# First batch's row sums and bias turn moved behind the high turn of token tile 2; the last product, its eviction and its store cut into two column halves

## The reference

```
x = x + tanh(g_xattn) * (fq(layernorm(x)) @ fq(ctx))             # fq: quantize to 0..255 and back
x = x + tanh(g_ffn)   * ffn(layernorm(x))
ffn(t):  gate = the 2 best of 16 experts for each row, from 2 of 4 groups, softmax scores + bias
         y    = sum over experts of gate_e * ((silu(t@w1_e + b1_e) * (t@w2_e + b2_e)) @ w3_e + b3_e)
         z    = (silu(t@sw1 + sb1) * (t@sw2 + sb2)) @ sw3 + sb3  # shared expert, 512 wide
         return y + z
```

## Time and profile before

| what | value |
|---|---|
| median of 3 runs | 316.2 us (315.91 to 316.38) |
| the profiled execution's own time | 316.27 us |
| its span | 314.3 us |
| PE busy | 293.9 us (94%) |
| DVE busy | 222.8 us (71%) |
| ACT busy | 114.9 us (37%) |
| mean granted TensorE clock | 0.998 of full speed |

### The profile page before, as it was taken

One profiled execution on the slowest core, in us unless ns is written; L12 is line 12 of the kernel. 1 busy time (PEld: TensorE's weight loads), 2 busy tenths in 40 slices (PEclk: granted clock), 3 DMA queues, 4 the chain that ended last, 5 costly groups with the idle time before them and its releaser, 6 DMA issues.

```text
span 314.3 us, 4647 instructions
## 1 busy us (share of the span) xinstructions
PE 293.9 (94%) x1868; PEld 149.4 (48%) x1868; DVE 222.8 (71%) x392; ACT 114.9 (37%) x130; POOL 24.3 (8%) x34
## 2 busy tenths in 40 slices
PE   0388999999999999999999999999999999999993
PEld 0224598954544445544444444444444444444441
DVE  2898987895898953685475988868784769659110
ACT  2998558769653540210343305302015040100000
POOL 2010200000002210000000011100101110000000
PEclk9999999999999999999999999999999999999999
DMA  7999970248710753000897600000000000600302
GB/s 277 413 325 346 301 219 6 82 136 168 230 60 0 136 106 95 2 2 0 250 306 250 229 39 2 0 0 0 2 0 0 2 1 0 255 15 1 133 33 104
DMA packets 35700, 35.56 MB, mean 113 GB/s; under 512 B 16068, under 2 KB 30428, under 8 KB 35548
## 3 DMA queue, kind: packets, MB, share of 16 engines
q1 hardware_dynamic: 35664, 35.23, 36.0%
q10 hardware_dynamic: 12, 0.00, 0.0%
HBM read 27.88 MB, written 4.20 MB: 102 GB/s over the span
## 4 chain that ended last, share of the span: by engine, by line
PE 83%; DVE 9%; DMA 3%; ACT 2%; SPq 1%; POOL 1%; issue 1%; DVEq 0%
PE PS L1532 26%; PE PS L1374 20%; PE PS L1565 12%; PE PS L1558 7%; PE PS L1409 7%; PE PS L1321 4%; DMA X<-in_x_dram 3%; PE PS L1390 2%; DVE stats L778 2%; PE PS L1398 2%; PE PS L1328 1%; DVE S2f L814 1%; POOL lnR L474 1%; DVE X L844 1%; DVE wrow L853 1%; DVE area L810 1%
## 5 line engine op out<-in xcount | busy, mean ns | idle before, releaser
L1374 PE MATMUL PS<-areaT,areaW 128*128 128x512 f16 x288 | 62.6, 379 | 0.0
L1374 PEld LDWEIGHTS PS<-areaT,areaW 128*128 128x128 f16 x288 | 28.0, 98 | 33.3
L1532 PE MATMUL PS<-areaT,area 128*128 128x512 f16 x192 | 42.1, 379 | 0.0
L1532 PE MATMUL PS<-areaT,areaW 128*128 128x512 f16 x192 | 42.1, 379 | 0.0
L1321 PE MATMUL PS<-area,areaQ 128*128 128x512 f16 x128 | 32.0, 400 | 1.6 <-DVE area L810 1.5
L1042 DVE SCALAR_TENSOR_TENSOR X<-PS,cf,X 128x512 f32<-128x512 f32 x22 | 15.5, 746 | 20.0 <-PE PS L1565 15.2
L1532 PEld LDWEIGHTS PS<-areaT,area 128*128 128x128 f16 x192 | 18.8, 98 | 22.7
L1532 PEld LDWEIGHTS PS<-areaT,areaW 128*128 128x128 f16 x192 | 18.8, 98 | 22.7
L778 DVE BATCH_NORM_STATS2 stats<-X 128x6 f32<-128x512 f32 x32 | 20.5, 683 | 4.5 <-DMA X<-in_x_dram 4.3
L1558 PE MATMUL PS<-SW,areaH 128*128 128x512 f16 x96 | 21.9, 379 | 0.0
L1321 PEld LDWEIGHTS PS<-area,areaQ 128*128 128x128 f16 x128 | 12.6, 102 | 17.8 <-DVE area L810 3.6
(11 more groups left out here) (187 smaller groups left out, 408.6 us busy)
## 6 DMA issues: line engine op xcount, KB each, us to landing
areaT<-in_ctx_dram SPq DMA_DIRECT2D x12, 512.0 KB, 8.1
ring<-in_L_ffn_sw_dram SPq DMA_DIRECT2D x12, 512.0 KB, 5.5
X<-in_x_dram SPq DMA_DIRECT2D x8, 512.0 KB, 7.6
ring<-in_L_ffn_ew_dram SPq DMA_DIRECT2D x16, 256.0 KB, 5.6
out_dram<-X SPq DMA_DIRECT2D x7, 512.0 KB, 2.7
ring<-in_ctx_dram SPq DMA_DIRECT2D x4, 512.0 KB, 3.8
ring<-in_L_ffn_ew_dram SPq DMA_DIRECT2D x2, 1024.0 KB, 5.0
areaQ<-gate_dram SPq DMA_DIRECT2D x1, 1024.0 KB, 6.8
```

Of the source, the lines that this page charges most:

```text
L1374: last = mm(PS[:, SU_BANK[half * SC + c] + w, lo:hi], SW[:, wp, 2 * c + w, k, :], XT[:, xp, k, tk], start=(k == 0 and n == 0), stop=(k == ...
L1532: last = mm(PS[:, EU_BANK[u] + w, :], W12S[j][:, wp, k, cs], XT[:, xp, k, b * S:(b + 1) * S], start=(k == 0 and n == 0), stop=(k == KC - 1 ...
```

## The change

1. On PE, `bias_columns` and `row_sums(0)` leave their place between the products of tile 2 (after k = 3) and are called in `transpose_tokens(2)`, between the high and the low turn. They wait for `at_read` 4 (the eviction of tile 3, which frees bank 3) in place of `q1_rdy`. PE no longer waits for `r1_rdy` and `sbT_rdy` before the products of tile 3.
2. On DVE, `row_terms(0)` and `shared_biases()` move from behind `attend(1)` to behind `ln2_lo(3)`; at the end of `shared_biases` DVE waits for its own two writes. `su_silu_of(0)` on ACT waits for them too, and the first DMA turn of the second batch (`turn_q1(4)`) also waits for the row sums.
3. The product `P3` of pair 1 of the second batch becomes two groups of 18 matmuls with 256 columns (`last_product`), the first in its old bank, the second in the next one (bank 4), each with a semaphore.
4. DVE evicts the two halves one by one (`last_halves`).
5. The stores of the last two tiles are five instead of three: the first 512 columns of tile 4 and of tile 5 as soon as `X11f` is done, the last 512 of tile 4 after `X12f` of pair 0, and the last 512 of tile 5 in two of 256 columns.

```
-            sp.wait_ge(y_rdy, evict_no(1, "X11f", 1))
-            store(TB + 1, slice(0, 512))
+            for pair in range(2):
+                sp.wait_ge(y_rdy, evict_no(1, "X11f", pair))
+                store(TB + pair, slice(0, 512))
             sp.wait_ge(y_rdy, evict_no(1, "X12f", 0))
-            store(TB)
+            store(TB, slice(512, D))
+            sp.wait_ge(y_first, 1)
+            store(TB + 1, slice(512, 768))
             sp.wait_ge(y_rdy, evict_no(1, "X12f", 1))
-            store(TB + 1, slice(512, D))
+            store(TB + 1, slice(768, D))
...
             attend(1)
-            row_terms(0)
-            shared_biases()
             lo_chunk("sw", 0)
...
             ln2_lo(3)
+            row_terms(0)
+            shared_biases()
             lo_chunk("sw", 4)
...
             def row_sums(b):
-                if b == 0:
-                    pe.wait_ge(q1_rdy, TB)
-                else:
+                if b:
                     for j in range(2):
                         pe.wait_ge(q1t_in[j], 32)
-                    pe.wait_ge(at_read, TB)
+                    pe.wait_ge(r1_rdy, 1)
+                    pe.wait_ge(sbT_rdy, 2)
...
                 pe.wait_ge(sbr_in, 32)
+                pe.wait_ge(at_read, TB)
                 nc.tensor.transpose(PS[:, 3, 8:16], sbr[:, :], idf[0:8, 0:8]).then_inc(sb_T, 1)
...
                 last.then_inc(tk_T, 1)
+                if i == 2:
+                    bias_columns()
+                    row_sums(0)
                 pe.wait_ge(ln_lo, i + 1)
...
                 products(2, k)
-                if k == 3:
-                    pe.wait_ge(q1_rdy, TB)
-                    bias_columns()
-                    row_sums(0)
             column_sums(2)
-            pe.wait_ge(r1_rdy, 1)
-            pe.wait_ge(sbT_rdy, 2)
+            pe.wait_ge(q1_rdy, TB)
...
+            def last_halves(x):
+
+                dve.wait_ge(y_rdy, evict_no(1, "X12u", 1))
+                dve.wait_ge(dn_first, 1)
+                v.scalar_tensor_tensor(x[:, 0:256], PS[:, bank_of(1, "P3", 1), 0:256], cf[:, 11:12], x[:, 0:256], ALU.mult,
+                                       ALU.add).then_inc(y_first, 1)
+                dve.wait_ge(dn_done, STEPS)
+                v.scalar_tensor_tensor(x[:, 256:512], PS[:, LAST_BANK, 0:256], cf[:, 11:12], x[:, 256:512], ALU.mult,
+                                       ALU.add).then_inc(y_rdy, 1)
...
+            def last_product():
+
+                piece, blk = PRODUCT["P3"]
+                free_bank(1, "P3", 1)
+                for half, bank in enumerate((bank_of(1, "P3", 1), LAST_BANK)):
+                    if half:
+                        pe.wait_ge(y_rdy, evict_no(1, READ_LAST["P5"], 0))
+                    o, cs = PS[:, bank, 0:256], slice(half * 256, half * 256 + 256)
+                    for c in range(SC):
+                        for n, (hp, wp) in enumerate(((0, 0), (1, 0), (0, 1))):
+                            mm(o, HT[:, hp, c, P:2 * P], SW3[:, wp, c, 512 + half * 256:768 + half * 256],
+                               start=(c == 0 and n == 0), stop=False)
+                    for c in range(HC):
+                        a = pieces(1, 0, c, PIECE[piece], 1), pieces(1, 1, c, PIECE[piece], 1)
+                        for n, (hp, wp) in enumerate(((0, 0), (1, 0), (0, 1))):
+                            last = mm(o, a[hp][:, 0, 1, :], W3B[BLOCK[blk]][:, wp, c, cs], start=False,
+                                      stop=(c == HC - 1 and n == 2))
+                    last.then_inc(dn_done if half else dn_first, 1)
...
-            for pair in range(2):
-                product(1, "P3", pair, (pair, 1))
+            product(1, "P3", 0, (0, 1))
+            last_product()
```

More of the change, by code:

```diff
@@ L188, in build @@
         EVICTIONS = 2 * (len(EVICT[0]) + len(EVICT[1]))
-        STORES = NT + 1
+        STORES = NT + 3
         U = ring[:, :, :].rearrange("p a n -> p (a n)").rearrange("p (u n) -> p u n", n=512)
@@ L202, in bank_of @@
             return (6, 7, 0, 1, 2, 3, 4, 5)[(step_no(b, name, pair) - 1) % 8]
+        LAST_BANK = (6, 7, 0, 1, 2, 3, 4, 5)[STEPS % 8]
         WROW = [wrow[:, i % 2, :] for i in range(NT)]
@@ L240, in build @@
         u0_rdy = sem("u0_rdy")
+        dn_first, y_first = sem("dn_first"), sem("y_first")
         dn_done, y_rdy, y_out, rows_fin = sem("dn_done"), sem("y_rdy"), sem("y_out"), sem("rows_fin")
@@ L330, in turn_q1 @@
                     sp.wait_ge(at_done, TB)
+                    sp.wait_ge(r1_done, 1)
                 sp.dma_start_transpose(Q1T[:, i % TB, :, :], QB[:, i % 2, :]).then_inc(q1t_in[i % 2], 16)
@@ L580, in su_silu_of @@
                 act.wait_ge(su_done, u + 1)
+                if u == 0:
+                    act.wait_ge(sbT_rdy, 2)
                 if u >= 2:
@@ L838, in shared_biases @@
                 v.tensor_scalar(sbT[:, 1, :], PS[:, 3, 8 + SC:8 + 2 * SC], UPS, None, ALU.mult).then_inc(sbT_rdy, 1)
+                dve.wait_ge(sbT_rdy, 2)
             def attend(i):
@@ L1080, in evictions @@
                     from_bank(b, "X11f", p, x11[p], "P2", x11[p], "X11u")
-                for p in range(2):
+                for p in range(2 - b):
                     from_bank(b, "X12f", p, x12[p], "P3", x12[p], "X12u")
+                if b:
+                    last_halves(x12[1])
             dve.wait_ge(x_in[0], 16)
```

## The result

The changed kernel takes 313.72 us (median of 6 runs, 313.35 to 314.19), the kernel before 315.85 us in the runs beside it (6 runs, 314.88 to 316.38). The ratio is 0.9934, with a 95% interval from 0.9917 to 0.9952: 0.66% faster. The forecast was 314.3 us, in a range from 313.2 to 315.7.

A forecast was written before the change was run, and what follows sets the result against it. PE bounds the kernel, with DVE's chain setting tile 2's low turn. PE's end at 308.67 (308.97 - 0.34 + 0.04) plus 3.63 behind it gives 312.3 of span, plus 1.97 outside: 314.3 us, range 313.2 to 315.7.

The forecast's parts named there:

- The move, DVE's side: Three small reads leave DVE's chain ahead of tile 2's low turn, where they take 0.34 us.
- The move, PE's side: Bias turn and row sums fit before tile 2's low turn with 0.16 us to spare; PE's list moves by -0.34 us.
- The halves: Last product on PE: 36 matmuls of 256 columns for 18 of 512, +0.04 us; PE's end at 308.67.
- The last eviction: Behind the last matmul: 256 columns take 479 ns instead of 745, -0.27 us.
- The last store: Kernel's end: store meets the branch's first instruction fetch, not the second; 3.6 us behind PE's end in place of 5.33.
- The queue reads further ahead: Rival: read-ahead well over 36 instructions, branch and fetches earlier, last store undisturbed; 313.3 us, chance 0.12.
- The store stays disturbed: Rival: last store's packets still wait behind a later fetch; 315.7 us, or 315.0 with half the gain; chance 0.14.
- The branch comes late: Rival: wait between halves stops PE's read-ahead, register read only at PE's end; 316.3 us, or 316.9; chance 0.07.
- The move gives nothing: Rival: PE's lead lost at tile 2's low turn, +0.11 for -0.34 us, all else as forecast; 314.7 us, chance 0.08.
- the 0.86 for faster: Chance of faster by over 0.2% (below 315.6 us): 0.59 + 0.12 + 0.08 + most of the disturbed store.

The follow-up runs named there:

- the run with the second sums: Changed kernel with the 32 row sums run a second time at their old place on PE, result unused; 313.94 us, 0.9929 of before.
- the late branch: Changed kernel with one more wait on PE, for its own last matmul, ahead of the register read; 315.64 us, 1.0003 of before.
- quarters: Changed kernel with the last product in four groups of 128 columns in four banks, evicted one by one; 314.70 us, 0.9959 of before.
- the whole product and the new stores: Changed kernel with last product and eviction whole, and four stores of 512 columns; 315.47 us, 1.0011 of before.

## Why the prediction was right, and where not

**The move, DVE's side: mechanism right, size 0.25 instead of 0.34.** The three reads left the chain: `lo_chunk` starts 33.13 - 31.82 = 1.31 us behind the second eviction's start in place of 33.56 - 31.91 = 1.65. But `ln2_lo(0)` now starts at 34.34, when ACT's second write ends (33.08 + 1.23 = 34.31), 2.52 us after the second eviction's start instead of 34.69 - 31.91 = 2.78 in the kernel before: 0.08 of the 0.34 went to a wait for ACT that DVE's own work had covered. The kernel before at this place:

```profile
31.91 1.28 DVE L844 SCALAR_TENSOR_TENSOR X<-PS,cf,X 128x1024 f32<-128x1024 f32 x1
33.18 1.23 ACT L564 ACTIVATE rows<-X,lnB,lnA 128x1024 f32<-128x1024 f32 x1
34.69 1.22 DVE L853 TENSOR_TENSOR wrow<-rows,wrow 128x1024 f16<-128x1024 f32 x1
```

**The move, PE's side: right.** The moved work doesn't wait for the eviction of tile 3, the lead is 0.62 us (forecast 0.61), and the sums leave room of 0.16 us, as forecast, by the 0.82 us that the run with the second sums gives them. That the room agrees to the hundredth is luck: the bias turn starts 49.20 - 48.66 = 0.54 us behind the high turn's start, 0.09 more than the text's 0.45, and DVE comes 0.09 later too. The turn that binds first is not that of tile 1, as the text says, but that of tile 0, where PE now waits 0.16 us; it changes nothing, since tile 1 binds after it:

```profile
35.63 0.62 PE L1387 MATMUL PS<-idh,wrow 128*128 128x128 f16 x8 [0.16 <-DVE wrow L863]
```

**The halves: right.** 24 + 12 matmuls took from 304.57 to 308.67, where 35 steps of 0.109 us and the last one's 0.27 give 4.09 us. PE's end was forecast at 308.67 and is 308.67 in the profiled run (it hides that this execution started 0.09 us earlier and the move gave 0.09 less).

**The last eviction: right**, 484 ns for 479.

**The last store: right in the cause, the term too large.** The text put 3.63 us behind PE's end; it is 311.5 - 308.67 = 2.83. The register read came at 306.6 (forecast 306.52), the branch at 307.6 (307.42), the fetch at 308.6 (308.35). But I took the fetch's 1.88 us and the hold of 4.28 from the kernel before, where the fetch lay in a store of 512 KB. Here it lies in no store and takes 1.06 us, the hold is 3.57, and so the last store isn't disturbed at all: 0.8 us less. That is most of the difference between 314.3 and the profiled run's 313.35; over all runs of the changed kernel the median is 313.72. (The hold was 3.43 to 3.87 us in the six runs whose fetch lay between two stores or behind the last, so what sets it is open.) That the gain of the medians, 2.13 us, is near the forecast's 2.0 is in part luck: from trace to trace the span lost 2.8, and the trace of the kernel before, on which the forecast was built, is of an execution near its slow end. The Trainium skill (Runtime: NRT & Kernel Launch, Instruction fetch mechanics) says that a taken branch out of the pages held has to fetch its target before going on; the run of the kernel before without its branch agrees (no fetch in the last 9 us), and so does the one with the late branch (2.4 us of waiting for PE).

**The rivals.** *The queue reads further ahead* gave nearly the right time (313.3) and the undisturbed last store for the wrong reason: the register is read where the last 18 loads and 18 matmuls begin, for whole product, halves and quarters alike (304.9, 306.6, 307.6). *The store stays disturbed* is what the quarters do. *The branch comes late* is what the extra wait does, at nearly the price forecast (5.0 us behind PE's end for 5.7). *The move gives nothing* holds in time when it is made alone, but not in any trace. In the chances, the 0.86 for faster holds 0.07 of the disturbed store's 0.14 beside 0.59, 0.12 and 0.08: half of it, not most.

**What PE's queue counts.** At the end of the list each last group has 18 loads and 18 matmuls and a wait in front, so these rows alone don't say whether the queue reads ahead by a count or up to that wait. The trace of the kernel before does say it, in the shared expert, whose groups have 24 matmuls 0.2158 us apart and each a wait in front. In front of the third and the fourth group stands one more wait (L1371), an instruction of PE's queue by itself:

```profile
64.66 20.88 PE L1374 MATMUL PS<-areaT,areaW 128*128 128x512 f16 x96
...
L1371 PEldq EVENT_SEMAPHORE  x2: 51/51/51, 71.2 to 76.3; - x2
```

The two groups begin at 64.66 + 48 x 0.2158 = 75.0 and at 80.2 us. So the queue is at both waits 3.9 us, that is 18 matmuls with their loads, ahead, in the middle of the group before and past that group's own wait. Here it is a count, of about 36 instructions.

**What stays open.** Why the move alone comes out at 1.0013, with the low turn 0.25 us earlier. Its end is the disturbed one, and where the fetches fall against the last store decides over a microsecond; that the move shifts them to a worse place was not tried. What sets a fetch's length is open as well (below).

## What to carry to other kernels

Look at what the engine that ends last does behind its last instruction: a taken branch at the end of a list was reached here some 18 matmuls ahead of the engine, so the length of these matmuls decided when the fetch ran, and whether it met the last store. Cutting the last product shortens eviction and store, but it also brings the branch nearer to the end: halves win here, quarters lose. And a move that only fills idle time is worth what it takes from the chain that ends the wait, no more.

## What was not expected

- A fetch of PE's instructions (0.02 MB) took 0.98 and 1.06 us of a DMA engine in the changed kernel, in no store, but 1.88 in a store of 512 KB and 1.59 in one of 256. It isn't only the store: with the whole product and the new stores a fetch in a store of 256 KB took 1.13 us (70.8% of 0.1 us x 16), with the quarters one in the last store 1.05; and in no store one took 1.17 with the late branch and 1.19 with the sums twice.
- The halves bring one more fetch, at 304.5, ahead of the branch; the runs with halves and no branch have it too, the kernel before without its branch has none there. The list is 36 instructions longer. It fell between two stores and cost nothing here.
- The kernel before spreads over 2.3 us and more (314.59 to 316.85 in 29 runs of one comparison), the one without its branch over 1.0 (313.69 to 314.71, 9 runs), the changed one over 0.8 (6 runs).
